# Gated delta-rule attention on one core: the correction of a triangular inverse summed in one bank, the unit matrix taken off by VectorE, and the inverse's steps moved

## Chip, core and metric

One core of a Trainium2 chip runs the whole program. The metric is device microseconds from start to end. One profiled execution gives the rows below; its own time stands beside its span in the table of the section on the profile.

## What is computed

The input has 2 sequences of 512 tokens, 256 wide. The first layer is linear attention with a gated delta rule: 16 key heads, 2 value heads to each, 128 wide. Cut to its core, the reference does for each value head and token

```python
def step(Sst, inp):
    q_t, k_t, v_t, g_t, beta_t = inp
    Sst = Sst * jnp.exp(g_t)[..., None, None]
    kv = jnp.einsum('bhk,bhkv->bhv', k_t, Sst)
    delta = (v_t - kv) * beta_t[..., None]
    Sst = Sst + k_t[..., None] * delta[:, :, None, :]
    o = jnp.einsum('bhk,bhkv->bhv', q_t, Sst)
    return (Sst, o)
```

Before it come a projection, a causal convolution of 4 taps and SiLU; behind it a normalisation, a gate SiLU(z) and an output projection. The second layer is a mixture of 12 experts, which the change doesn't touch.

## The kernel before

**Tiling.** Tokens are cut into chunks of 128, 4 to a sequence. For a key head there are 16 units (2 sequences, 4 chunks, 2 value heads), each with a 128 x 128 unit-triangular matrix A. The delta rule inside a chunk is a solve with A; the kernel makes an inverse Z of A and multiplies with it. A head is one pass of the whole program, and the units are worked in 4 groups of 4 (`g` 0 to 3, one PSUM bank of 512 columns each) or in 2 halves of 8.

**The inverse.** `aT` is A transposed; `aH` (fp16) and `aL` (the rest) are its parts. `st` starts an approximate inverse X0, `y`, `p` and `turn` widen it in 5 levels, with Z0 its transpose. Then comes one correction of higher order, which the change is about. With R the residual (unit matrix less A X0), Z = Z0 + R Z0 + R (R Z0):

- `res` (`residual`, L631 on TensorE): for each of the 4 units of a group, aH X0 + aL X0 (L640, L641) and a third product (L642) that takes the unit matrix off: `minus16` times `ident16`. ScalarE (L873) copies the bank with scale −1 to fp16, `res0`. VectorE (L1083) makes `res1`, the part that fp16 leaves out, in bf16.
- `once` (`apply_once`, L645): res0 Z0 into a bank of its own (L651); ScalarE (L877) copies it to fp16.
- `Z` (`finish_z`, L654): into a further bank, four products for each unit: res0 `once`, res1 Z0, res0 Z0 again, and the unit matrix times Z0 (L660 to L663). ScalarE (L881) copies it to `Z` in fp32.

**The recurrence.** For chunks c = 0 to 3 in turn: `ks c` (products with the state St, TensorE L687; VectorE L1094 makes `rh` of it), `solve c` (Z times rh, L704; ScalarE L904 copies to `dl`), `su c` (L713; VectorE updates St, L1102 for c = 0 and L1108), `pdl` and `qs` for the output.

**Order.** Every engine runs its steps in one written order: `FIRST`, then `ORDER` once for each of the heads 1 to 12, then `LAST` (L39 to L276). An entry (a, step, x) of `ORDER` is done for head w + a, so that three heads overlap. `run` gives each engine those entries that it has a part in, in the order of the list. `BANK` gives the PSUM bank of each step (banks 2 to 7). `full` and `free` of a bank count its uses; `is_full` waits until TensorE has filled it, `is_free` until its reader is done. Semaphores beside them count the tiles in SBUF (`res_high`: res0 is made).

**VectorE's order around the change.** In a head of `ORDER`, with the heads' number left out: `p (2,1)`, `y (4,0)`, `tap 1`, `y (3,1)`, `pdl 3`, `p (4,0)`, `sum 2`, `sum 3`, `norm`, `p (3,1)`, `tap 2`, `weigh 0`, `tok 0`, `tok 1`, `y (4,1)`, `weigh 1`, `p (4,1)`, `tap 3`, `weigh 2`, `weigh 3`, `res 0`, `op 0`, `tap 0`, `res 1`, `op 1`, `res 2`, `op 2`, `op 3`, `kk 0`, `aT 0`, `kk 1`, `aT 1`, `split z`, `split out`, `res 3`, `kk 2`, `st 0`, `su 0`, `st 1`, `aT 2`, `ks 1`. The lines: `tap` is L1023, `weigh` L1143, `op` L1150, `kk` L1054 (mask of a bank), `aT` L1060 (the factor: kkm times decay, both in SBUF), `split z` L1007, `split out` L1013 (fp32 weights less their fp16 part, both in SBUF), `st` L1066, `y` L1072, `p` L1081. TensorE's order from `ks 1` on: `ks 1`, `y (0,0)`, `x0 0`, `kk 3`, `solve 1`, `once 3`, `p (0,0)`, `qs 1`, `st 2`, `su 1`, and so on to `y (2,1)`, `turn (1,1)`, `p (3,0)`, `proj 1`, `p (2,1)`. GpSimd's: `gl 3`, `pT 0` (L1187, from kkm and decay), `unit 0`, `unit 1` (L1193, writes ones on the diagonal of aT), `aL 0` (L1199, the low part), `pT 1`, `aL 1`, `unit 2`, ...; `unit g` waits for the factor `aT g`, `aL g` for ScalarE's aH, and `aT 2` comes in VectorE's order behind `st 1`.

## Time and profile before

| | us |
|---|---|
| Runs: median of 3 (lowest, highest) | 1452.8 (1451.58, 1452.94) |
| The profiled execution's own time | 1452.13 |
| Its span, first to last instruction | 1450.4 |
| TensorE busy | 1386.4 (96%) |
| VectorE busy | 1085.8 (75%) |
| ScalarE busy | 1049.7 (72%) |
| GpSimd busy | 697.1 (48%) |
| Attention, about | 0 to 1104 |

PE is TensorE, PEld its weight load, DVE VectorE, ACT ScalarE, POOL GpSimd. A row of a group gives the line, engine, operation, output and inputs with shapes, how often, busy time and the mean of one in ns, and behind the second bar the idle time before. Matmul rows overlap their neighbours, since a matmul's row runs to the end of its pipeline; the distance of two starts is what it takes of the engine. A VectorE row of 0.68 us also overlaps the next by some 0.09.

### The profile page before, as it was taken

The numbers are of one execution on the slowest core, as the hardware profiler recorded it, in microseconds if no ns is written. First come the engines' busy times: TensorE is split into PE (matmuls) and PEld (weight loads), VectorE is DVE, ScalarE is ACT, GpSimd is POOL, SyncE is SP. The second block draws the span as 40 slices with busy tenths as digits, with TensorE's granted clock in tenths as the row PEclk, the third lists the DMA queues.
The fourth block names the chain that finished last, engine by engine and source line by source line (L and its number), as shares of the span: only waits on it lengthen the run. The fifth ranks groups of instructions, "written<-read, shape, count | busy, mean of one in ns | idle before, by whom it ended". The sixth has DMA issues, their size and how long they took to land.

```text
span 1450.4 us, 36480 instructions
## 1 busy us (share of the span) xinstructions
PE 1386.4 (96%) x14236; PEld 1114.9 (77%) x14236; DVE 1085.8 (75%) x1926; ACT 1049.7 (72%) x2114; POOL 697.1 (48%) x619
## 2 busy tenths in 40 slices
PE   5689999999999999999999999999978999999996
PEld 3568888898888889798888979888865567667676
DVE  5678999999999999999999999998865512213225
ACT  5777887878788787878888887887755465564651
POOL 0545555446564545556454555545315454353440
PEclk8899999999999999999999999999998999999998
DMA  3000202011020211102030110201131112112100
GB/s 118 16 1 2 67 3 58 24 38 38 24 60 2 60 24 38 38 25 59 2 60 18 44 38 24 60 2 39 32 101 39 56 37 73 38 37 73 37 1 29
DMA packets 100992, 55.76 MB, mean 38 GB/s; under 512 B 74572, under 2 KB 93016, under 8 KB 100824
## 3 DMA queue, kind: packets, MB, share of 16 engines
q1 hardware_dynamic: 100824, 53.43, 14.2%
q8 instruction: 116, 1.90, 0.5%
q14 instruction: 52, 0.43, 0.1%
HBM read 35.59 MB, written 1.05 MB: 25 GB/s over the span
## 4 chain that ended last, share of the span: by engine, by line
PE 89%; DVE 5%; ACT 2%; issue 2%; DMA 1%; POOL 0%; SPq 0%; POOLq 0%; DVEq 0%; ACTq 0%
PE bank L532 11%; PE bank L1486 11%; PE bank L1469 11%; PE bank L687 6%; PE bank L733 5%; PE bank L674 5%; PE bank L704 4%; PE bank L722 4%; PE bank L713 3%; PE bank L622 2%; PE bank L614 2%; PE bank L630 2%; PE bank L582 2%; PE bank L558 2%; PE bank L583 2%; DVE con L1023 2%
## 5 line engine op out<-in xcount | busy, mean ns | idle before, releaser
L1023 DVE SCALAR_TENSOR_TENSOR con<-bank,taps,con 128x1022 f32<-128x1022 f32 (+2 forms) x192 | 245.4, 1278 | 19.9 <-ACT con L802 15.3
L1808 POOL TENSOR_TENSOR h<-h 128x512 f16<-128x512 f32 x120 | 142.5, 1192 | 159.7 <-ACT h L1586 147.7
L532 PE MATMUL bank<-x,qkv 128*128 128x512 f16 x768 | 183.5, 390 | 6.5 <-DVE con L1023 6.5
L1179 POOL TENSOR_TENSOR gl<-const_sb,gc 128x512 f16<-128x512 f32 x128 | 129.9, 1040 | 120.3 <-DVE gc L1033 75.2
L1585 ACT ACTIVATE h<-bank,b 128x512 f32<-128x512 f32 x120 | 82.5, 687 | 119.0 <-PE bank L1469 115.8
L1469 PE MATMUL bank<-y,w 128*128 128x512 f16 x720 | 163.2, 386 | 1.7 <-ACT h L1586 1.4
L1486 PE MATMUL bank<-w,h 128*128 128x256 f16 x1440 | 159.9, 273 | 0.0
L1486 PEld LDWEIGHTS bank<-w,h 128*128 128x128 f16 x1440 | 140.9, 98 | 18.4
L532 PEld LDWEIGHTS bank<-x,qkv 128*128 128x128 f16 x768 | 73.4, 100 | 88.5 <-issue 8.7
L1469 PEld LDWEIGHTS bank<-y,w 128*128 128x128 f16 x720 | 70.2, 99 | 90.6 <-ACT h L1586 8.1
L1214 POOL TENSOR_TENSOR oo<-oo 128x512 f16<-128x512 f32 x64 | 74.2, 1170 | 122.0 <-ACT oo L930 122.0
L1081 DVE TENSOR_TENSOR X<-X,bank 128x512 f16<-128x512 f16 x160 | 109.0, 682 | 16.1 <-PE bank L622 14.7
L1399 DVE SCALAR_TENSOR_TENSOR w<-w,w 128x1280 f16<-128x1280 f32 x12 | 17.8, 1490 | 134.1 <-ACT w L1387 134.1
L871 ACT ACTIVATE Z<-bank 128x512 f16<-128x512 f32 x160 | 96.4, 604 | 23.7 <-PE bank L630 23.7
L1072 DVE TENSOR_TENSOR Y<-bank,ymask 128x512 f16<-128x512 f32 x160 | 109.4, 685 | 2.9 <-PE bank L614 2.3
L802 ACT ACTIVATE con<-bank,taps 128x512 f32<-128x512 f32 x128 | 85.4, 687 | 30.8 <-PE bank L532 30.6
L1206 POOL TENSOR_TENSOR kd<-k_tok,gc 128x512 f32<-128x512 f32 x48 | 50.0, 1043 | 112.0 <-PE bank L713 112.0
L733 PE MATMUL bank<-out,sqo 128*128 128x256 f16 x768 | 96.7, 277 | 7.2 <-ACT zs L889 5.5
L1187 POOL TENSOR_TENSOR pT<-kkm,decay 128x512 f32<-128x512 f32 x64 | 88.0, 1376 | 17.4 <-issue 12.8
L1709 DVE SCALAR_TENSOR_TENSOR facc<-bank,gcol,facc 128x256 f32<-128x256 f32 x88 | 38.5, 479 | 76.6 <-PE bank L1486 76.6
L674 PE MATMUL bank<-z,x 128*128 128x256 f16 x768 | 89.6, 273 | 1.4 <-ACT zs L889 0.8
L733 PEld LDWEIGHTS bank<-out,sqo 128*128 128x128 f16 x768 | 73.3, 99 | 22.1 <-issue 8.7
(222 smaller groups left out, 3858.2 us busy)
## 6 DMA issues: line engine op xcount, KB each, us to landing
w<-in_w SPq DMA_DIRECT2D x24, 640.0 KB, 4.4
w_qkv<-in_W_qkvz SPq DMA_DIRECT2D x16, 512.0 KB, 4.3
w_out<-in_W_out SPq DMA_DIRECT2D x16, 256.0 KB, 3.0
w_z<-in_W_qkvz SPq DMA_DIRECT2D x16, 256.0 KB, 2.9
Z<-in_xT SPq DMA_DIRECT2D x2, 512.0 KB, 5.5
y<-in_x SPq DMA_DIRECT2D x1, 1024.0 KB, 7.8
sqo<-oo SPq DMA_TRANSPOSE x64, 2.7
out_dram<-y SPq DMA_DIRECT2D x8, 128.0 KB, 1.8
```

The source lines that it names most:

```text
L532: last = mm(bank[:, b], qkv16[:, w, a, t * P:(t + 1) * P], x16[:, x, a, b * S:(b + 1) * S], start=(a == k == 0), stop=(a == HT - 1 and k = ...
L674: last = mm(out[:, j * 256:(j + 1) * 256], x16[:, x, a, m * P:(m + 1) * P], z16[:, w, a, :], start=(a == k == 0), stop=(a == HT - 1 and k ...
L733: last = mm(out[:, j * H:(j + 1) * H], oT[:, g % 2, o, 2 * j + r], out16[:, w, r, :], start=(r == i == 0), stop=(r == R - 1 and i == len(P ...
L871: freed(do(dst, src, ACT.Copy), "turn", lh)
L1023: stt(out=out, in0=bank[:, 0:B, 0:S - k], scalar=taps[:, par, t, TAPS - 1 - k:TAPS - k], in1=out, op0=ALU.mult, op1=ALU.add).then_inc(tap_ ...
L1072: freed(tt(Y[:, h], at_bank("y", lh).rearrange("p (u k) -> p u k", u=8), ymask[:, l].unsqueeze(1).broadcast_to([P, 8, P // 2]), ALU.mult), ...
L1081: freed(tt(x, x, at_bank("p", lh).rearrange("p (q b) -> p q b", b=b), ALU.subtract), "p", lh)
L1179: last = tt(gl[:, g % 2, k].rearrange("p (m r) d -> p m r d", m=2), upper.unsqueeze(1).unsqueeze(1).broadcast_to([P, 2, R, P]), gc[:, par, ...
L1187: tt(pT[:, par, 4 * g:4 * g + 4].rearrange("p (m r) d -> p m r d", m=2), kkm[:, g % 2, :, 1].unsqueeze(2).broadcast_to([P, 2, R, P]), deca ...
L1469: last = mm(h_bank(n, k), w1_16[:, n % 2, w, a, t * P:(t + 1) * P], y16[:, x, a, h * S:(h + 1) * S], start=(a == i == 0), stop=(a == HT - ...
L1486: last = mm(o_bank(k)[:, j * H:(j + 1) * H], h16[:, n % 2, h, t, m * P:(m + 1) * P], w2_16[:, n % 2, w, t, :], start=(t == i == 0), stop=( ...
L1808: tt(h16[:, n % 2, 1, t, at], h32[:, k % H32], h16[:, n % 2, 0, t, at], ALU.subtract).then_inc(h_low, 1)
```

## The change

Six things change.

1. TensorE's `residual` leaves out the product with `minus16`: 2 products for a unit instead of 3.
2. VectorE makes `res0` itself, with one instruction that scales the bank by −1 and adds the unit matrix (fp16, broadcast over the 4 units), and waits for it (`res_high`) before `res1` from the same bank. `res1` is −(A X0) less res0 as before, so it now differs from R's rest by the unit matrix. ScalarE's `residual` is gone.
3. The correction is summed in the bank of `once`. `apply_once` starts it (only its first product has the start flag), ScalarE copies R Z0 out, and `finish_z` adds to the same bank: res0 `once`, res1 Z0, and `twice16` (twice the unit matrix) times Z0; the second unit matrix answers to what `res1` now has too little of. The second res0 Z0 is left out: 3 products for a unit instead of 4.
4. `Z` needs no bank of its own, so four entries of `BANK` go, and `p (4,1)` and `once 2` get other banks.
5. Semaphores `once_ready` and `z_full`, four of each, take the place of bank waits between these steps.
6. The orders are rewritten. In `ORDER`, VectorE's steps differ in two places: `res 1` comes before `tap 0`, and `res 3` between `aT 0` and `kk 1` instead of behind `split out`. On TensorE, `res 1` comes before `proj 0`, `once 2` behind `op 3`, `res 3` right behind `kk 0`, `Z 2` and `once 1` behind `kk 1`, `Z 3` before `st 3`, `y (4,1)` before `z 1`, `y (3,1)` before `decay 0`, `turn (1,0)` behind `y (2,0)`. On ScalarE, `once 2` is last, and `v (1,1)` comes before `turn (1,0)`. GpSimd's and the DMA queue's orders stay, but for the list's cut (`aL 3` is first of a head instead of last of the one before). `FIRST` and `LAST` are rewritten more widely, in the same manner.

```diff
@@ ORDER: the entries around the moved steps
-    (1, "aT", 1), (0, "split", "z"), (0, "split", "out"), (0, "Z", 2),
-    (0, "once", 1), (0, "res", 3), (1, "aH", 0), (1, "kk", 2),
...
+    (0, "res", 3), (1, "kk", 1), (1, "aT", 1), (0, "split", "z"),
+    (0, "split", "out"), (0, "Z", 2), (0, "once", 1), (1, "aH", 0),
...
@@ tensor: residual, apply_once, finish_z, solve
                 mm(out[:, at], aH[:, u], X0[:, u], start=True, stop=False)
-                mm(out[:, at], aL[:, u], X0[:, u], start=False, stop=False)
-                last = mm(out[:, at], minus16[:], ident16[:], start=False, stop=True)
+                last = mm(out[:, at], aL[:, u], X0[:, u], start=False, stop=True)
             filled(last, "res", g)
...
             for j in range(4):
-                last = mm(out[:, j * P:(j + 1) * P], res0[:, g, j], Z0[:, 4 * g + j], start=True, stop=True)
+                last = mm(out[:, j * P:(j + 1) * P], res0[:, g, j], Z0[:, 4 * g + j], start=(j == 0), stop=True,
+                          skip_group_check=True)
             filled(last, "once", g)
...
-            is_free(pe, n, ("res", g), ("once", g), taking=("Z", g))
-            out = take(n, "Z", g)
+            pe.wait_ge(once_ready[g], n + 1)
+            is_free(pe, n, ("res", g))
+            out = at_bank("once", g)
             for j in range(4):
                 u, at = 4 * g + j, slice(j * P, (j + 1) * P)
-                mm(out[:, at], res0[:, g, j], once[:, g % 2, j], start=True, stop=False)
-                mm(out[:, at], res1[:, g, j], Z0[:, u], start=False, stop=False)
-                mm(out[:, at], res0[:, g, j], Z0[:, u], start=False, stop=False)
-                last = mm(out[:, at], ident16[:], Z0[:, u], start=False, stop=True)
-            filled(last, "Z", g)
+                mm(out[:, at], res0[:, g, j], once[:, g % 2, j], start=False, stop=False, skip_group_check=True)
+                mm(out[:, at], res1[:, g, j], Z0[:, u], start=False, stop=False, skip_group_check=True)
+                last = mm(out[:, at], twice16[:], Z0[:, u], start=False, stop=True, skip_group_check=True)
+            last.then_inc(z_full[g], 1)
...
-                needs += [("Z", c // 2), ("Z", 2 + c // 2)]
+                needs += [("once", c // 2), ("once", 2 + c // 2)]
@@ scalar
         def turn_start(n, par, h):
-            is_full(act, n, ("x0", h), ("Z", 2 * h, 1), ("Z", 2 * h + 1, 1))
+            is_full(act, n, ("x0", h))
+            if after(n, 1):
+                act.wait_ge(z_full[2 * h], n)
+                act.wait_ge(z_full[2 * h + 1], n)
...
-        def residual(n, par, g):
-            is_full(act, n, ("res", g), ("Z", g, 1))
-            do(res0[:, g], quads(at_bank("res", g)), ACT.Copy, scale=-1.0).then_inc(res_high, 1)
-
         def apply_once(n, par, g):
-            is_full(act, n, ("once", g), ("Z", g - 2) if g >= 2 else ("Z", g + 2, 1))
-            freed(do(once[:, g % 2], quads(at_bank("once", g)), ACT.Copy), "once", g)
+            is_full(act, n, ("once", g))
+            if g >= 2:
+                act.wait_ge(z_full[g - 2], n + 1)
+            elif after(n, 1):
+                act.wait_ge(z_full[g + 2], n)
+            do(once[:, g % 2], quads(at_bank("once", g)), ACT.Copy).then_inc(once_ready[g], 1)
 
         def finish_z(n, par, g):
-            is_full(act, n, ("Z", g), ("solve", 2 * (g % 2) + 1, 1))
-            freed(do(Z[:, 4 * g:4 * g + 4], quads(at_bank("Z", g)), ACT.Copy), "Z", g)
+            act.wait_ge(z_full[g], n + 1)
+            is_full(act, n, ("solve", 2 * (g % 2) + 1, 1))
+            freed(do(Z[:, 4 * g:4 * g + 4], quads(at_bank("once", g)), ACT.Copy), "once", g)
@@ vector
-            ts(minus16[:], ident, -1.0, None, ALU.mult)
+            ts(twice16[:], ident, 2.0, None, ALU.mult)
...
         def residual(n, par, g):
+            is_full(dve, n, ("res", g))
+            if after(n, 1):
+                dve.wait_ge(z_full[g], n)
+            stt(out=res0[:, g], in0=quads(at_bank("res", g)), scalar=-1.0,
+                in1=ident16[:].unsqueeze(1).broadcast_to([P, 4, P]), op0=ALU.mult, op1=ALU.add).then_inc(res_high, 1)
             dve.wait_ge(res_high, 4 * n + g + 1)
             freed(stt(out=res1[:, g], in0=quads(at_bank("res", g)), scalar=-1.0, in1=res0[:, g],
                       op0=ALU.mult, op1=ALU.subtract), "res", g)
```

## Rows read from the trace of the kernel before

**Rows 1.** The page, part 1: busy time, share and count.
```profile
PE 1386.4 (96%) x14236; PEld 1114.9 (77%) x14236; DVE 1085.8 (75%) x1926; ACT 1049.7 (72%) x2114; POOL 697.1 (48%) x619
```

**Rows 2.** Busy time by stretches: length, engines, granted clock, DMA share, GB/s.
```profile
400.60:464.50 63.90, 63.78 (x747) 54.72 (x745) 59.74 (x105) 52.50 (x114) 34.12 (x31) 1.00 0.14 35
...
976.00:1040.00 64.00, 62.71 (x760) 54.99 (x759) 56.44 (x107) 49.36 (x109) 28.26 (x25) 1.00 0.11 27
```

**Rows 3.** Groups by line, whole span: products that go, ScalarE's step, its neighbour.
```profile
L662 PE MATMUL bank<-Z,res 128*128 128x128 f16 x256 | 56.1, 219 | 0.0
...
L642 PE MATMUL bank<-ident,minus 128*128 128x128 f16 x256 | 46.0, 219 | 0.0
...
L1085 DVE SCALAR_TENSOR_TENSOR res<-bank,res 128x512 bf16<-128x512 f32 x64 | 43.4, 683 | 10.1 <-ACT res L875 10.1
...
L875 ACT ACTIVATE res<-bank 128x512 f16<-128x512 f32 x64 | 38.6, 603 | 13.1 <-PE bank L642 12.6
```

**Rows 4.** TensorE in order of time: start us, duration us, what.
```profile
416.70 0.22 PE L640 MATMUL bank<-X,aH 128*128 128x128 f16 x1
...
417.31 0.22 PE L642 MATMUL bank<-ident,minus 128*128 128x128 f16 x1
...
433.34 1.03 PE L687 MATMUL bank<-St,kT 128*128 128x256 f32 x4
...
455.66 0.40 PE L622 MATMUL bank<-Y,Z 128*128 128x64 f16 x8
```

**Rows 5.** VectorE in order of time, with the waits.
```profile
415.91 0.69 DVE L1085 SCALAR_TENSOR_TENSOR res<-bank,res 128x512 bf16<-128x512 f32 x1 [0.51 <-ACT res L875]
...
417.58 3.91 DVE L1023 SCALAR_TENSOR_TENSOR con<-bank,taps,con 128x1022 f32<-128x1022 f32 x3 [0.38 <-ACT con L802]
...
424.64 0.69 DVE L1054 TENSOR_TENSOR kkm<-bank,const_sb 128x512 f32<-128x512 f32 x1 [0.16 <-PE bank L583]
425.37 0.69 DVE L1060 TENSOR_TENSOR aT<-kkm,decay 128x512 f32<-128x512 f32 x1
425.98 0.68 DVE L1054 TENSOR_TENSOR kkm<-bank,const_sb 128x512 f32<-128x512 f32 x1
426.69 1.05 DVE L1060 TENSOR_TENSOR aT<-kkm,decay 128x512 f32<-128x512 f32 x1
427.67 1.12 DVE L1007 SCALAR_TENSOR_TENSOR z<-w_z,z 128x512 f16<-128x512 f32 x1
428.71 1.12 DVE L1013 SCALAR_TENSOR_TENSOR out<-w_out,normw,out 128x512 f16<-128x512 f32 x1
429.75 0.68 DVE L1085 SCALAR_TENSOR_TENSOR res<-bank,res 128x512 bf16<-128x512 f32 x1
430.35 0.67 DVE L1054 TENSOR_TENSOR kkm<-bank,const_sb 128x512 f32<-128x512 f32 x1
...
431.94 0.69 DVE L1102 COPY St<-bank 128x512 f32<-128x512 f32 x1 [0.25 <-PE bank L713]
...
433.14 0.68 DVE L1060 TENSOR_TENSOR aT<-kkm,decay 128x512 f32<-128x512 f32 x1
434.40 1.13 DVE L1094 SCALAR_TENSOR_TENSOR rh<-bank,gc,v_tok 128x128 f32<-128x128 f32 x4 [0.58 <-PE bank L687]
...
456.09 0.69 DVE L1081 TENSOR_TENSOR X<-X,bank 128x512 f16<-128x512 f16 x1 [0.47 <-PE bank L622]
```

**Rows 6.** GpSimd in order of time over the same steps.
```profile
425.47 1.73 POOL L1187 TENSOR_TENSOR pT<-kkm,decay 128x512 f32<-128x512 f32 x1 [0.91 <-issue]
427.14 2.13 POOL L1193 TENSOR_SCALAR_AFFINE_SELECT aT<-aT 128x512 f32<-128x512 f32 x2
429.25 1.59 POOL L1199 TENSOR_TENSOR aL<-aT,aH 128x512 f16<-128x512 f32 x1
...
432.03 1.16 POOL L1199 TENSOR_TENSOR aL<-aT,aH 128x512 f16<-128x512 f32 x1
```

**Rows 7.** The z split's line alone: durations ns min/median/max over 16 heads.
```profile
L1007 DVE SCALAR_TENSOR_TENSOR z<-w_z,z x16: 681/1118/1445, 98.2 to 1073.2; 128x512 f16<-128x512 f32 x16
```

More of the change, by code:

```diff
@@ new lines @@
+    (15, "load", "out"), (14, "sum", 1), (14, "sqo", 2), (14, "solve", 3),
+    (14, "sum", 2), (15, "turn", (3, 0)), (15, "turn", (2, 1)), (15, "y", (3, 1)),
[3 rows of a table added]
+    (14, "weigh", 0), (15, "turn", (3, 1)), (14, "z", 2), (14, "weigh", 1),
+    (14, "high", 0), (14, "weigh", 2), (14, "z", 3), (15, "norm", 0),
+    (14, "high", 1), (15, "p", (4, 1)), (14, "high", 2), (15, "turn", (4, 0)),
+    (15, "res", 0), (15, "res", 1), (15, "pT", 3), (15, "turn", (4, 1)),
[4 rows of a table added]
+    (14, "low", 0), (15, "once", 1), (14, "op", 2), (14, "high", 3),
@@ L323, in attention @@
     pT = sb("pT", [P, 2, U, P])
-    minus16 = sb("minus16", [P, P], F16)
+    twice16 = sb("twice16", [P, P], F16)
     unit_cols = sb("unit_cols", [P, LEVELS, P // 2], F16)
@@ L370, in attention @@
         "proj_full", "tap0_done", "tap_done", "silu_done", "sq_done", "rs_ready"))
+    once_ready, z_full = ([sem(f"{name}{g}") for g in range(4)] for name in ("once_ready", "z_full"))
     scaled = sem("scaled")
```

201 lines of the change are left out of this document (107 added, 94 removed), and 236 rows, old and new, of tables (BANK, FIRST, LAST, ORDER).

## Prediction

> **What bounds the kernel now.** I read the views from wide to narrow: the page, then busy time by stretches, then the groups by line, then the order in time of TensorE, VectorE and GpSimd over one head. The page puts TensorE at 96% of the span [rows 1]. By stretches [rows 2], the middle of the kernel repeats every 63.9 us: the stretch shown is one of 13 alike between 145 and 976 us. TensorE is busy 63.78 of 63.90 us there at a granted clock of 1.00 (its 2.4 GHz level), and VectorE 59.74 us. So TensorE is the bound of a head and VectorE is only 4 us behind. In the last full stretch but one of attention, 976 to 1040 us, both have a little room. The experts (from 1104 us on) are not touched.
>
> **What goes from TensorE.** In `residual` the product with `minus16`, in `finish_z` the second product of res0 with Z0: 4 each per step, 4 steps a head, 16 heads, 512 products of 128 columns [rows 3]. Their price is not the 219 ns of a row, which overlap, but the distance of starts: from the first product of a `res` step to its twelfth there are 11 steps in 0.61 us [rows 4], 55.6 ns each. A head saves 32 x 0.0556 = 1.78 us, the kernel 28.5 us, if TensorE stays the bound. By the Trainium skill (TensorE: Matmul & The Clock Gate, Back-to-back issue gap) pairs of load and matmul of 128 columns are sustained at about 81 ns, which would make it 41.5 us; the rows are shorter, and they decide.
>
> **What moves.** ScalarE loses `residual`, 64 x 0.60 us [rows 3]; it is busy 52.5 us a head [rows 2] and only waits less. VectorE gets that step as a `scalar_tensor_tensor` of one bank. Nothing in the trace is this very instruction; the nearest row is L1085, same engine and opcode, same bank and 512 elements, 0.68 us [rows 3]. In its queue such an instruction takes less, since the next starts before it ends (429.75 to 430.35, 0.60), but its partner res1 needs its result at once. That is the spacing of the mask product and the factor behind it, 425.98 to 426.69, 0.71 us [rows 5]. I take 0.71; 0.60 is the low end and 1.1 (a blocked instruction, 428.71 below) the high end. Four a head: **+2.84 us**, 2.4 to 4.4. `twice16` for `minus16` and the flags of the products cost nothing: same instructions, same count. The extra pair of waits on z_full is met long before: a Z step stands most of a head ahead of the next `res` of its group. Evacuations of `once` and `Z` are the same instructions from one bank instead of two.
>
> **Where that lies.** VectorE needs 59.7 + 2.8 = 62.5 us a head and TensorE 62.1: they are now equals, and what counts is how they hand over. The loop of a head that sets the end has three pieces, in the clock of [rows 4] and [rows 5].
> (a) VectorE's own queue, from the instruction `p (2,1)` that waits for TensorE at 456.09 to the state copy at 431.94 of the next head (495.84): 39.75 us. VectorE waits four times in it: 0.51, 0.38, 0.16 and, at the copy itself, 0.25.
> (b) From the copy to the `ks 1` products that read the state, 433.34: 1.40 us, of which the copy is 0.69. The rest is TensorE's queue.
> (c) TensorE's queue from `ks 1` to `p (2,1)` at 455.66, and 0.43 to VectorE's start: 22.75 us.
> Together 63.90.
> In (a) all four `res` pairs lie, +2.84. With VectorE late, its four waits go: 1.30, and 0.09 more for each (0.69 of duration against 0.60 of spacing), 1.66. Moving `res 3` ahead of `kk 1` and taking ScalarE's part out remove the wait for ScalarE. Net +1.18, so the copy is no longer waiting for the products of `su 0`, and TensorE, now about 1.5 us ahead, waits for the copy: (b) falls to 0.69 + 0.06 = 0.75, −0.65. (c) loses the four products of `Z 3`: −0.22. `once 2`, moved behind `op 3`, will wait about a microsecond for res0, which falls in TensorE's spare time. Sum so far +0.31, a head of 64.2.
>
> **The port.** There is one more term in (a). The second factor `aT` takes 1.05 us at 426.69, and the two weight splits 1.12 each at 427.67 and 428.71 [rows 5]; the same z split takes 0.68 when nothing runs beside it [rows 7]. All three read two operands from SBUF. Each begins while a GpSimd instruction is under way, the pT product (425.47) and the two unit selects (427.14) [rows 6], and ends some 0.55 us after that one: whoever starts first holds the other up. Factors that start ahead of GpSimd (425.37) take 0.69. L1085 and the mask products read one bank and at most one SBUF operand, and never stretch, so the new instruction doesn't either. The Trainium skill says the same (SBUF — State Buffer, Who interferes with whom): a VectorE instruction with two SBUF inputs and a GpSimd one that reads SBUF block each other for a whole instruction, by order of issue. The trace agrees, with 1.12 against 0.68.
> In the new order `res 3` (1.31 us) stands between the first factor and `kk 1`. GpSimd finishes pT and the first select before the second factor starts (pT 426.3 to 428.0, select to 428.6, factor 428.8), so that takes 0.69; the z split starts right behind it, before the second select that waits for the factor, and takes 0.68; the out split is still blocked. **−0.36 −0.44 = −0.80**. The loop: 63.90 + 0.31 − 0.80 = **63.4 us a head**; over 13 heads −6.4 us.
>
> **The ends.** Attention's first 145 us and last 128 us hold three heads' work outside this loop, with a rewritten order. Saved products are worth at most 3 x 1.78 = 5.3 us there; added VectorE work costs at most 3 x 2.84 = 8.5. From 976 to 1040 us VectorE is busy 56.4 us of 64 [rows 2], so products saved in head 14 and in head 15 up to its first solve should show by about half of 3.6: I take −2, ends −5.3 and +4. The three solves behind them alternate between engines and don't change. Sum: −6.4 − 2 = −8.4 us on the profiled execution's 1452.1 us, 1443.7; the median of runs stands 0.7 us above that execution, so **1444 us**.
>
> **Rivals.**
> 1. *TensorE stays the bound.* All 28.5 us come off: 1424. For it: TensorE is full now. Against: VectorE's 62.5 us leave no room for heads of 62.1 us. 0.06, with 0.05 for cases in between.
> 2. *The relief at the port is given back one instruction later.* With pT, the selects and the low parts about 1.3 us later on GpSimd than now ([rows 6]: low parts at 429.25 and 432.03), its second low part starts at about 433.3, and the factor `aT 2`, which now starts at 433.14 clear of it, would start at 433.5 and wait a whole low part: 1.5 us instead of 0.69. That puts `ks 1`'s evacuation and `solve 1` some 0.6 us later: 64.0 us a head, +1.3 over 13, with the ends and the median's 0.7 1452. It hangs on 0.2 us. 0.19.
> 3. *Slower: VectorE's queue is the bound and the port gives nothing.* From the place between `res 0` and `ks 1`, +0.31 a head as summed above, or +0.9 with rival 2 on top: 1452.8 + 4 = 1457 up to 1465. It decides as soon as the port gives back less than 0.31 us a head. For it: 2.84 us go to the engine with 4 us left, and those four microseconds are mostly waits that the recurrence forces (0.58 before `ks 1` [rows 5]). The Trainium skill warns of this side (Perfetto Trace Analysis, Optimizing Scalar/DVE Operations): with VectorE saturated, work should go to ScalarE, and the change goes the other way. 0.25.
> That the change doesn't do what it says can be told by counts alone, and I see no way for it.
>
> **How the numbers follow.** Forecast 0.46; partial cases between it and rival 1 0.05; rival 1 0.06; rival 2 0.19; rival 3 0.24. Faster by over 0.2% (2.9 us, about what a measurement can tell): the forecast, the partial cases and rival 1, 0.57. Within 0.2%: rival 2, 0.19. Slower: rival 3, 0.24. The forecast's own range is 1438 to 1449 (ends ±4, port ±0.1 a head). To leave out 2 in 10 the range takes in rivals 2 and the nearer part of 3 and leaves out rival 1: 1434 to 1459.
>
> **What would show it.** Right: heads of 63.4 us; TensorE busy near 62 us a head with gaps in front of `once 2` and `ks 1`; VectorE without waits from `p (2,1)` to the state copy; the new instruction at 0.68 and 0.71 ahead of res1; the second factor and the z split at 0.69; `aT 2` at 0.68. Wrong in size: any of the three SBUF products at 1.05 or more. Wrong in kind: heads of 62.1 us with VectorE still waiting, or TensorE's gaps at another step than those two.

## Result, and the profile after

The kernel became slower: median 1471.2 us (1469.34 to 1471.79, 4 runs) against 1452.6 us of the kernel before in the same comparison, a ratio of 1.0128 [1.0112, 1.0144]. The forecast of 1444 and its range, 1434 to 1459, both missed. The profiled execution took 1471.79 us, its span 1470.0 us, 19.6 us more than before.

The page's line of busy times, which answers to [rows 1], and the shares of the chain that ended last, by engine:

```profile
PE 1369.1 (93%) x13724; PEld 1087.7 (74%) x13724; DVE 1132.2 (77%) x1990; ACT 1020.9 (69%) x2050; POOL 691.6 (47%) x619
...
PE 62%; DVE 22%; issue 8%; ACT 6%; POOL 1%; DMA 1%; SPq 0%; DVEq 0%; POOLq 0%; ACTq 0%
```

The same line of the chain in the kernel before:

```profile
PE 89%; DVE 5%; ACT 2%; issue 2%; DMA 1%; POOL 0%; SPq 0%; POOLq 0%; DVEq 0%; ACTq 0%
```

The counts are those of the diff: 512 products fewer on TensorE, 64 instructions more on VectorE and 64 fewer on ScalarE. What changed in kind is the chain: it ran through TensorE for 89% of the span and now passes from engine to engine.

**Where the 19.6 us are.** One row per head tells it, VectorE's first copy of the state, whose instruction waits for the recurrence. It first runs at 111.66 us before and 118.55 after: +6.9 in the opening. From this copy to the last one (15 distances, opening and closing heads among them) it is 945.0 us before and 959.1 after: +14.1. Behind the last copy it is −1.30. A middle head, 63.90 before, is 65.12, where 63.4 was forecast. (For every kernel below I give these two figures, first copy and middle head.)

The stretches of [rows 2] again, start and end, then length, then busy time of PE, PEld, DVE, ACT, POOL, then the granted clock, DMA share and GB/s:

```profile
0.00:80.00 80.00, 51.48 (x379) 34.96 (x379) 46.92 (x71) 50.57 (x90) 24.90 (x30) 0.83 0.19 61
80.00:145.00 65.00, 56.86 (x607) 44.72 (x607) 52.15 (x84) 43.90 (x97) 25.24 (x26) 0.92 0.02 6
400.60:464.50 63.90, 61.45 (x700) 51.91 (x697) 61.68 (x106) 50.42 (x109) 33.60 (x30) 1.00 0.16 35
```

TensorE is now idle 2.45 us in these 63.9, and VectorE is as busy as TensorE. TensorE in order of time, those rows of one middle head that have a wait in front of them (in brackets, us and what ended it), and two that mark the loop's pieces:

```profile
415.45 0.39 PE L615 MATMUL bank<-X,aH 128*128 128x64 f16 x8 [0.96 <-ACT Z L875]
...
422.30 1.48 PE L675 MATMUL bank<-z,x 128*128 128x256 f16 x12 [0.31 <-DVE X L1086]
...
433.59 1.47 PE L734 MATMUL bank<-out,sqo 128*128 128x256 f16 x12 [0.78 <-ACT Z L888]
...
441.74 1.13 PE L705 MATMUL bank<-v_tok,Z 128*128 128x128 f32 x8 [0.40 <-DVE kkm L1059]
...
446.58 1.03 PE L688 MATMUL bank<-St,kT 128*128 128x256 f32 x4
```

Four waits stand where the kernel before had hardly any, and none of them is where the prediction put one (`once 2` and `ks 1`). They are `y (4,1)`, `z 3`, `op 2` and `solve 0`. Each waits for a bank whose reader has not yet come to it: `y (4,1)` needs bank 2, which held `turn (4,0)` (ScalarE's L875 reads it); `z 3` needs bank 4 of `p (4,1)`; `op 2` needs bank 2, which `once 0` now keeps until `Z 0` is out; `solve 0` needs bank 4 of `kk 1`, whose mask VectorE now makes behind `res 3`.

VectorE in order of time over the same head; it answers to [rows 5]:

```profile
403.88 0.69 DVE L1086 TENSOR_TENSOR X<-X,bank 128x512 f16<-128x512 f16 x1 [0.47 <-PE bank L623]
...
419.43 2.00 DVE L1153 SCALAR_TENSOR_TENSOR oo<-oo,rso,zs 128x128 f32<-128x128 f32 x4
421.56 0.69 DVE L1086 TENSOR_TENSOR X<-X,bank 128x512 f16<-128x512 f16 x1
...
428.08 0.69 DVE L1092 SCALAR_TENSOR_TENSOR res<-bank,ident 128x512 f16<-128x512 f32 x1
428.80 0.69 DVE L1095 SCALAR_TENSOR_TENSOR res<-bank,res 128x512 bf16<-128x512 f32 x1
...
441.63 0.69 DVE L1065 TENSOR_TENSOR aT<-kkm,decay 128x512 f32<-128x512 f32 x1
442.24 0.69 DVE L1012 SCALAR_TENSOR_TENSOR z<-w_z,z 128x512 f16<-128x512 f32 x1
442.84 1.12 DVE L1018 SCALAR_TENSOR_TENSOR out<-w_out,normw,out 128x512 f16<-128x512 f32 x1
...
445.18 0.69 DVE L1112 COPY St<-bank 128x512 f32<-128x512 f32 x1
...
446.39 1.50 DVE L1065 TENSOR_TENSOR aT<-kkm,decay 128x512 f32<-128x512 f32 x1
```

The loop's pieces in these rows, beside the forecast: (a) from `p (2,1)` at 403.88 to the state copy at 445.18 it is 41.30 us (40.13 forecast); (b) from there to `ks 1` at 446.58 it is 1.40 (0.75 forecast); (c) from `ks 1` to the next `p (2,1)`, 469.01, it is 22.43 (22.53 forecast). Their sum is 65.13.

The row that stands out is 2.00 us for `weigh 1`. The row of GpSimd beside it, and the row of ScalarE on which `y (4,1)` waited:

```profile
414.65 0.65 ACT L875 ACTIVATE Z<-bank 128x512 f16<-128x512 f32 x1
...
419.33 1.16 POOL L1224 TENSOR_TENSOR oo<-oo 128x512 f16<-128x512 f32 x1 [2.28 <-ACT oo L935]
```

GpSimd's low part of `oo` starts 0.10 us ahead of `weigh 1`, and `weigh 1` takes 2.00 in place of 1.13. The ScalarE copy at 414.65 stands right behind the eight squares of `sq1`. So the suspicion was a chain: `y (4,1)`, moved ahead of `z 1`, waits 0.96 us for bank 2; `z 1` and all behind it (`high 0`, then GpSimd's `low 0`) come late; `low 0` meets `weigh 1`.

The first half of this holds, and the second half costs nothing. The chain that ended last, in order of time (start, us, what; the same head), leads from ScalarE's copy through TensorE's own queue to VectorE's `p (4,1)`, the row at 421.56, and leaves `weigh 1` out:

```profile
414.82 0.50 ACT Z L875
...
415.45 0.39 PE bank L615 x8
415.84 2.62 PE bank L675 x24
...
421.29 0.25 PE bank L623 x8
421.56 0.69 DVE X L1086
```

`weigh 1` ends at 421.43, and VectorE then still waits 0.13 us for TensorE's `p (4,1)`. Without the collision it would have waited 1.00 us there. So what makes the head longer is TensorE's wait, which reaches `p (4,1)` undiminished; the 2.00 us are hidden behind it.

### The profile page after: what moved, and what is told of

Read it like the earlier page. It is cut to its first block, busy times and chain, and to the rows that moved or that the text cites. A ratio compares the mean times of both kernels' runs of the same rounds, so it can differ in the third digit from the quotient of the medians.

```text
span 1470.0 us, 35518 instructions
## 1 busy us (share of the span) xinstructions
PE 1369.1 (93%) x13724; PEld 1087.7 (74%) x13724; DVE 1132.2 (77%) x1990; ACT 1020.9 (69%) x2050; POOL 691.6 (47%) x619
## 4 chain that ended last, share of the span: by engine, by line
PE 62%; DVE 22%; issue 8%; ACT 6%; POOL 1%; DMA 1%; SPq 0%; DVEq 0%; POOLq 0%; ACTq 0%
PE bank L1496 11%; PE bank L1479 10%; DVE con L1028 8%; PE bank L533 7%; PE bank L688 6%; PE bank L705 3%; PE bank L723 3%; PE bank L714 3%; PE bank L675 3%; PE bank L615 2%; DVE res L1092 2%; DVE y L1160 2%; PE bank L623 2%; DVE oo L1153 2%; ACT sq L825 2%
## 5 line engine op out<-in xcount | busy, mean ns | idle before, releaser
L1028 DVE SCALAR_TENSOR_TENSOR con<-bank,taps,con 128x1022 f32<-128x1022 f32 (+2 forms) x192 | 245.3, 1278 | 18.8 <-ACT con L803 14.1
L875 ACT ACTIVATE Z<-bank 128x512 f16<-128x512 f32 x160 | 96.5, 604 | 27.9 <-PE bank L631 27.9
```

The source lines that it names most:

```text
L875: freed(do(dst, src, ACT.Copy), "turn", lh)
L1028: stt(out=out, in0=bank[:, 0:B, 0:S - k], scalar=taps[:, par, t, TAPS - 1 - k:TAPS - k], in1=out, op0=ALU.mult, op1=ALU.add).then_inc(tap_ ...
```

## Experiments

Seventeen kernels ran beside the kernel before and the changed one. "Order" in the edits is the list `ORDER`, in which one entry stands for one step on all engines.

### The parts alone

**vector_only**: the kernel before, its orders and banks, with the VectorE part alone (`Z` keeps its own bank and the second product res0 Z0).

```diff
-                mm(out[:, at], aL[:, u], X0[:, u], start=False, stop=False)
-                last = mm(out[:, at], minus16[:], ident16[:], start=False, stop=True)
+                last = mm(out[:, at], aL[:, u], X0[:, u], start=False, stop=True)
@@ vector: residual, ahead of res1
+            stt(out=res0[:, g], in0=quads(at_bank("res", g)), scalar=-1.0,
+                in1=ident16[:].unsqueeze(1).broadcast_to([P, 4, P]), op0=ALU.mult, op1=ALU.add).then_inc(res_high, 1)
@@ scalar: residual is out; twos for ones in finish_z
```

> The kernel before with one part of the change: the product with the negative unit matrix goes, VectorE makes res0, ScalarE's step goes; order, banks and the four products of the Z step (the last with twice the unit matrix) as before. Theory 1 (load): VectorE's queue from p (2,1) to the state copy is on the loop that sets the end, and the 2.84 us a head put there come out less the waits they fill (1.66): heads of 64.3 to 65.2 us, 1457 to 1470 us in all. Theory 2 (order and bank): the loss comes from the rewritten order and from the bank that is held from the once step to the end of the Z step; neither is in this kernel, so that it stands at 1440 to 1453 us.

Measured: 1544.9 us, 1.0635 [1.0599, 1.0671]; first copy 113.51, heads of 69.4 and 70.5 us in turn. Neither theory came near it. TensorE in one of them:

```profile
455.52 0.60 PE L650 MATMUL bank<-Z,res 128*128 128x128 f16 x4 [4.00 <-DVE res L1080]
```

In the old order `once 2` comes soon after `res 2` on TensorE, while VectorE's `res 2` stands behind a tap step of 3.9 us. ScalarE had no such step in front of it. So the moves are no ornament: with the old order the VectorE part costs 92 us. But the run doesn't give this part's own price, since the wait drowns it.

**sum_only**: the changed kernel, its orders, banks and one-bank sum, with the residual as it was (product with `minus16`, ScalarE's copy).

```diff
-                last = mm(out[:, at], aL[:, u], X0[:, u], start=False, stop=True)
+                mm(out[:, at], aL[:, u], X0[:, u], start=False, stop=False)
+                last = mm(out[:, at], minus16[:], ident16[:], start=False, stop=True)
@@ scalar: residual is back; vector: the new instruction is out; ones for twos in finish_z
```

> The changed kernel (its order, its banks, the correction summed in one bank, three products in the Z step) with the old residual: product with the negative unit matrix, ScalarE makes res0. TensorE 0.89 us a head lighter than before, VectorE as before. Theory 1 (load): TensorE is the bound again, heads of 63.0 to 63.3 us, 1438 to 1446 us. Theory 2 (order and bank): the new waits stay, heads of 64 us and more, 1455 to 1470 us.

Measured: 1475.2 us, 1.0155 [1.0125, 1.0184]; first copy 118.81, heads 65.22. TensorE and VectorE of it:

```profile
414.97 0.39 PE L615 MATMUL bank<-X,aH 128*128 128x64 f16 x8 [0.94 <-ACT Z L876]
...
421.82 1.48 PE L676 MATMUL bank<-z,x 128*128 128x256 f16 x12 [0.31 <-DVE X L1093]
...
433.77 1.47 PE L735 MATMUL bank<-out,sqo 128*128 128x256 f16 x12 [0.78 <-ACT Z L895]
```

```profile
418.96 1.97 DVE L1155 SCALAR_TENSOR_TENSOR oo<-oo,rso,zs 128x128 f32<-128x128 f32 x4
```

This is the run that turned the inquiry. VectorE carries nothing new here, and the head and the opening are as long as in the changed kernel, with three of its four waits and the blocked `weigh 1`. The changed kernel's loss is in the orders and banks, and not in VectorE's load: putting that load back (changed kernel against sum_only) makes a head 0.10 us shorter. The chain that ended last leaves `weigh 1` out here too, and VectorE waits 0.14 us for `p (4,1)` behind it.

### Which move

**y41_back**: the changed kernel with `y (4,1)` back behind `z 2` in `ORDER`.

```diff
-    (0, "z", 0), (1, "y", (4, 1)), (0, "z", 1), (2, "silu", 2),
-    (0, "high", 0), (0, "z", 2), (0, "low", 0), (0, "low", 1),
-    (0, "oT", 3), (0, "weigh", 1), (1, "turn", (3, 1)), (2, "proj", 3),
+    (0, "z", 0), (0, "z", 1), (2, "silu", 2), (0, "high", 0),
+    (0, "z", 2), (0, "low", 0), (0, "low", 1), (0, "oT", 3),
+    (1, "y", (4, 1)), (0, "weigh", 1), (1, "turn", (3, 1)), (2, "proj", 3),
```

> The changed kernel with y (4,1) moved back behind z 2 in the twelve middle heads. In the changed kernel TensorE waits 0.96 us for ScalarE ahead of y (4,1), z 1 and the ScalarE and GpSimd steps behind it come late, and weigh 1 on VectorE starts 0.1 us behind a GpSimd instruction: 2.00 us instead of 1.13. If VectorE's queue is on the loop (theory 1): the collision goes, heads of 64.2 to 64.4 us instead of 65.1, 1458 to 1462 us. Rival: another engine is on the loop there, and the 0.87 us are hidden: 1470 us within 2.

Measured: 1457.2 us, 1.0036 [1.0018, 1.0054]; first copy 117.59, heads 64.03. One entry moved back returns 14 of the 18.6 us, 1.09 a head. (In the two traces 12.3 us of it lie between the first and the last copy. Another 1.0 lies ahead of the first copy, where the two kernels' lists are the same, so that part is not the move's.) VectorE of it, then TensorE:

```profile
399.38 0.69 DVE L1086 TENSOR_TENSOR X<-X,bank 128x512 f16<-128x512 f16 x1 [0.47 <-PE bank L623]
...
414.92 1.13 DVE L1153 SCALAR_TENSOR_TENSOR oo<-oo,rso,zs 128x128 f32<-128x128 f32 x4
...
439.59 0.69 DVE L1112 COPY St<-bank 128x512 f32<-128x512 f32 x1
```

```profile
436.15 1.13 PE L705 MATMUL bank<-v_tok,Z 128*128 128x128 f32 x8 [0.41 <-DVE kkm L1059]
...
440.99 1.03 PE L688 MATMUL bank<-St,kT 128*128 128x256 f32 x4
```

`weigh 1` is back at 1.13, and (a) is 40.21 us, where 40.13 was forecast. (b) is still 1.40. The gain is the distance from `p (2,1)` to `p (4,1)` on VectorE: 16.60 us, as in the kernel before, for 17.67 in the changed one. The expectation put it down to the collision; but the edit takes TensorE's wait away together with the collision, and by the chain above the wait is what counted.

**y41_forward**: the reverse test, the kernel before with that one entry moved forward and nothing else changed.

```diff
-    (0, "z", 1), (2, "silu", 2), (0, "high", 0), (0, "z", 2),
-    (0, "low", 0), (0, "low", 1), (0, "oT", 3), (1, "y", (4, 1)),
+    (1, "y", (4, 1)), (0, "z", 1), (2, "silu", 2), (0, "high", 0),
+    (0, "z", 2), (0, "low", 0), (0, "low", 1), (0, "oT", 3),
```

> The kernel before with y (4,1) ahead of z 1 in the middle heads and nothing else. Both y (4,1) and turn (4,0) use bank 2, and ScalarE copies turn (4,0) only behind the eight squares of sq1. If this wait is the cost in itself: TensorE loses 0.9 to 1.1 us a head, 1463 to 1467 us. If it costs only together with VectorE's added work: 1453 to 1456 us.

Measured: 1464.5 us, 1.0083 [1.0068, 1.0098]; heads 64.98, +1.08. TensorE, then VectorE and GpSimd:

```profile
408.99 0.39 PE L614 MATMUL bank<-X,aH 128*128 128x64 f16 x8 [0.95 <-ACT Z L871]
```

```profile
412.98 1.98 DVE L1143 SCALAR_TENSOR_TENSOR oo<-oo,rso,zs 128x128 f32<-128x128 f32 x4
```

```profile
412.87 1.16 POOL L1214 TENSOR_TENSOR oo<-oo 128x512 f16<-128x512 f32 x1 [2.27 <-ACT oo L930]
```

The same wait, the same collision with the same lead (0.11 us), the same price. With and without the rest of the change this move costs 1.1 us a head, as the first theory had it. Here too the chain that ended last goes through the ScalarE copy and TensorE and leaves `weigh 1` out, and VectorE waits 0.14 us for `p (4,1)` behind it. No kernel was run that has the wait and not the collision.

**res1_back**: the changed kernel with `res 1` back behind `tap 0`.

```diff
-    (1, "res", 1), (2, "proj", 0), (1, "once", 0), (2, "tap", 0),
+    (2, "proj", 0), (1, "once", 0), (2, "tap", 0), (1, "res", 1),
```

> The changed kernel with res 1 moved back behind tap 0 on both engines in the twelve middle heads. VectorE's work is the same, but tap 0, and with it silu 0, decay 1 and ScalarE's steps up to the state copy, come 1.3 us sooner. Theory 1a (VectorE's queue alone sets the loop): 1470 us within 2. Theory 1b (VectorE up to tap 0, then ScalarE's chain of silu 0, table load, decay 1 and the splits, sets it): heads about 0.6 us shorter, 1461 to 1465 us. If the move was right: slower, 1472 or more.

Measured: 1478.3 us, 1.0176 [1.0147, 1.0206]; heads 65.58, +0.46, with a new wait of 0.36 us for VectorE's `res` ahead of `op 3`. It comes out behind the changed kernel, so this move was right for that kernel.

### The waits that were left

**banks_free**, **banks_port** and **port_free** start from y41_back. The first gives `op 2`, `op 3`, `res 3` and `p (4,1)` other banks; port_free puts `aL 1` behind `unit 2` in `ORDER`, so that GpSimd's low part no longer holds up VectorE's `aT 2`; banks_port does both.

```diff
@@ banks_free
-    ("res", 3): 2 ... ("p", (4, 1)): 4 ... ("op", 2): 2 ... ("op", 3): 7
+    ("res", 3): 7 ... ("p", (4, 1)): 6 ... ("op", 2): 7 ... ("op", 3): 2
@@ port_free
-    (1, "pT", 1), (1, "aL", 1), (1, "y", (1, 0)), (0, "pdl", 1),
-    (1, "unit", 2), (1, "aH", 3), (2, "load", "qkv"), (1, "turn", (0, 0)),
+    (1, "pT", 1), (1, "y", (1, 0)), (0, "pdl", 1), (1, "unit", 2),
+    (1, "aL", 1), (1, "aH", 3), (2, "load", "qkv"), (1, "turn", (0, 0)),
```

> The changed kernel with y (4,1) behind z 2 (as in y41_back) and four banks exchanged: op 2 in bank 7 instead of 2 (which the once step of group 0 now holds until the Z step's copy), op 3 and res 3 in 2 and 7, p (4,1) in 6. TensorE's waits of 0.78 us ahead of op 2 and 0.35 ahead of z 3 go. If VectorE's queue from p (2,1) to the state copy is the bound of y41_back's heads (it shows no wait there in 40.2 us), they are hidden: heads of 63.8 to 64.05 us, 1454 to 1458 us. If TensorE's waits are what is lost: heads 0.8 to 1.1 us shorter, 1442 to 1448 us.

> banks_free with GpSimd's low part aL 1 moved behind unit 2, so that VectorE's aT 2 finds the port free (0.69 us instead of 1.50). If piece (b) of the loop can shrink only when both TensorE and VectorE come early (ks 1 right behind the state copy, its evacuation not behind a blocked aT 2): heads 0.3 to 0.7 us shorter than banks_free, 1446 to 1452 us. Rival: TensorE reaches ks 1 no sooner, and only 0.2 us a head are gained, 1453 to 1456 us.

> y41_back with aL 1 behind unit 2 alone, banks as changed. The price of aT 2 behind a GpSimd instruction by itself: its evacuation rh of ks 1 starts 2.62 us behind the state copy and could start at 2.46, when ks 1's products end. 0.2 us a head: 1454 to 1456 us against y41_back's 1457. If the blocked instruction cost its full 0.81 us: 1446.

Measured: 1469.0 us, 1.0106 [1.0087, 1.0125]; 1468.0 us, 1.0099 [1.0083, 1.0115]; 1458.5 us, 1.0037 [1.0024, 1.0051]. In all three a middle head stays at 64.03. In banks_free and banks_port the wait of `z 3` is gone. That of `op 2` has only changed its cause and grown: the profile now puts it down to the DMA that transposes its input. TensorE of banks_free:

```profile
426.77 1.49 PE L734 MATMUL bank<-out,sqo 128*128 128x256 f16 x12 [1.44 <-DMA sqo<-oo]
```

The head is no shorter without the first and no longer with the second: TensorE had that time to spare. The kernel as a whole lost 12 us by these banks, most of it in closing heads of 65.5 and 72.3 where y41_back has 63.6 and 65.6, and 3 us behind the last copy. And with `aT 2` unblocked, which the next rows show, nothing is gained either:

```profile
440.04 0.69 DVE L1112 COPY St<-bank 128x512 f32<-128x512 f32 x1
...
441.25 0.68 DVE L1065 TENSOR_TENSOR aT<-kkm,decay 128x512 f32<-128x512 f32 x1
442.51 1.12 DVE L1104 SCALAR_TENSOR_TENSOR rh<-bank,gc,v_tok 128x128 f32<-128x128 f32 x4 [0.58 <-PE bank L688]
```

The factor takes 0.68 instead of 1.50, and VectorE then waits 0.58 us for `ks 1` instead. The blocked factor had stood in a gap. For banks_free the head was forecast (63.8 to 64.05) and the whole was not; for banks_port and port_free even the smallest gain named did not come.

**solve_bank** (y41_back with `solve 0` in bank 3) takes the wait for `kk 1` away, and **solve_port** adds port_free's move to it.

```diff
-    ("solve", 0): 4, ("decay", 2): 7, ("st", 0): 2, ("su", 0): 4, ("st", 1): 5,
+    ("solve", 0): 3, ("decay", 2): 7, ("st", 0): 2, ("su", 0): 4, ("st", 1): 5,
```

> y41_back with solve 0 in bank 3 (free there once the Z copies it needs are made) instead of bank 4, where it waits 0.41 us for VectorE's mask of kk 1, which the change put behind res 3. Theory: the loop of y41_back's heads closes over this wait: kk 1 on VectorE, then TensorE's solve 0, decay 2, Z 1, st 0, su 0, pdl 0, decay 3, ks 1. Then ks 1 comes up to 0.4 us sooner, but its evacuation stays behind the blocked aT 2: 0.0 to 0.1 us a head, 1456 to 1458 us. If the blocked aT 2 doesn't hold: 0.3 to 0.5 a head, 1451 to 1453.

> solve_bank with aL 1 behind unit 2 on GpSimd, so that aT 2 isn't blocked. If both hold piece (b) of the loop together, only this one is shorter: heads of 63.5 to 63.7 us instead of 64.03, 1450 to 1453 us. If VectorE's queue with the ends of PE's work is the whole bound: 64.03 again, 1457 us.

Measured: 1458.4 us, 1.0041 [1.0025, 1.0057], heads 64.03; and 1456.0 us, 1.0024 [1.0014, 1.0034], heads 63.78. TensorE and VectorE of solve_port:

```profile
438.57 1.02 PE L688 MATMUL bank<-St,kT 128*128 128x256 f32 x4
```

```profile
437.32 0.68 DVE L1112 COPY St<-bank 128x512 f32<-128x512 f32 x1
...
439.63 1.13 DVE L1104 SCALAR_TENSOR_TENSOR rh<-bank,gc,v_tok 128x128 f32<-128x128 f32 x4 [0.44 <-PE bank L688]
```

Neither edit alone gives anything. In solve_bank (b) is already 1.25 and (a) 0.10 shorter, but (c) grows from 22.41 to 22.66, and `aT 2` freed takes that back. TensorE must be early for `ks 1` and VectorE free for what follows; both together give 0.25 us a head. Of the wait of 0.41 us ahead of `solve 0` about half is left, at `st 1` (0.22 us), which waits for VectorE's mask of `kk 2`. This is the best form of the whole change that I ran, and it is not faster than the kernel before.

### The one-bank sum without the VectorE part

**sum_banks**: sum_only with `y (4,1)` back and the banks of banks_free. **sum_lean**: the kernel before with its own orders and only the one-bank sum (`once 2` in bank 3, `op 2` in 5, `decay 1` in 2, and five steps moved in the opening and the closing where a bank forced it). **sum_lean2**: the same with two steps moved, for the waits that sum_lean showed: `split out` behind `res 3`, and `turn (4,1)` in bank 6 and, in opening and closing, later.

```diff
@@ sum_lean2 against sum_lean
-    (1, "aT", 1), (0, "split", "z"), (0, "split", "out"), (0, "Z", 2),
-    (0, "once", 1), (0, "res", 3), (1, "aH", 0), (1, "kk", 2),
+    (1, "aT", 1), (0, "split", "z"), (0, "Z", 2), (0, "once", 1),
+    (0, "res", 3), (0, "split", "out"), (1, "aH", 0), (1, "kk", 2),
```

> sum_only (old residual with ScalarE's res0, three products in the Z step) with y (4,1) behind z 2 and the same exchange of banks as banks_free. If the new waits of TensorE ahead of y (4,1), op 2 and z 3 were what made sum_only slow: TensorE is the bound with 63.0 us of work a head, heads of 63.1 to 63.6 us, 1444 to 1451 us with the seven us lost before the middle heads. If holding the bank costs elsewhere too: heads of 64 us, 1457 us or more.

> The kernel before (its orders and banks) with the sum in one bank alone: three products in the Z step instead of four, residual as before. Five steps moved in the opening and the end and none in the middle heads; once 2 in bank 3, op 2 in 5, decay 1 in 2, so that nobody waits for a bank that once holds. If the loss of sum_only came from the changed order and from op 2's bank: TensorE stays the bound with 0.89 us less a head: heads of 63.0 us, 1437 to 1442 us, faster than both. If holding the once bank or reading it twice costs in itself: heads of 63.5 or more, 1446 or more.

> sum_lean with turn (4,1) in bank 6 and ahead of op 1 in the opening and the end (instead of ahead of once 0), and with split out behind res 3 in the middle heads, so that VectorE reads res 3's bank a microsecond sooner and st 0 doesn't wait. If saved products are worth their spacing once no wait takes their place: heads of 63.0 to 63.2 us, 1440 to 1446 us, faster than both kernels. If something else holds the head: 63.6 again, 1449 us or more.

Measured: 1460.0 us, 1.0048 [1.0033, 1.0063], heads 63.43; 1457.8 us, 1.0037 [1.0023, 1.0051], heads 63.67; 1454.0 us, 1.0017 [1.0008, 1.0026], heads 63.66.

**What VectorE's part is worth.** sum_banks and banks_free have the same orders and banks and differ in the residual alone. The heads are 63.43 and 64.03, the whole 1460.0 and 1469.0 us: with these banks VectorE's part costs 0.60 us a head, all of it in (a), 39.61 against 40.22. With the banks of the change it costs nothing: sum_first (below) has heads of 64.14 where first_back and y41_back, with VectorE's part, have 64.03. The waits for banks had hidden it.

sum_banks has the shortest heads of all runs, as forecast, and not the time forecast with them: its first copy is at 118.58 us and its closing heads take up to 68.0.

**What the saved products are worth.** TensorE has 16 products, 0.89 us, less to do in a head, and the heads of the two lean kernels are 0.24 us shorter. In sum_lean (a) is 39.73 us, unchanged, and (c) is 22.53 for 22.75. That is the forecast's −0.22 for the four products of `Z 3`. The other twelve lie in (a) and give nothing, as TensorE and VectorE of sum_lean show:

```profile
437.27 0.38 PE L594 MATMUL bank<-ident,aH 128*128 128x128 f16 x4 [0.57 <-DVE res L1097]
```

```profile
438.64 0.69 DVE L1114 COPY St<-bank 128x512 f32<-128x512 f32 x1 [0.25 <-PE bank L715]
```

TensorE reaches `st 0` early and waits there for VectorE to empty the bank of `res 3`, so that the state copy behind it comes no sooner. All four waits of [rows 5] in (a) are still there. In sum_lean2, VectorE and then TensorE, the one at the copy is gone and the other three stay; the last row of VectorE is the first of them a head later:

```profile
418.31 0.69 DVE L1097 SCALAR_TENSOR_TENSOR res<-bank,res 128x512 bf16<-128x512 f32 x1 [0.52 <-ACT res L882]
...
419.99 3.91 DVE L1035 SCALAR_TENSOR_TENSOR con<-bank,taps,con 128x1022 f32<-128x1022 f32 x3 [0.39 <-ACT con L804]
...
427.04 0.69 DVE L1066 TENSOR_TENSOR kkm<-bank,const_sb 128x512 f32<-128x512 f32 x1 [0.16 <-PE bank L584]
...
481.97 0.69 DVE L1097 SCALAR_TENSOR_TENSOR res<-bank,res 128x512 bf16<-128x512 f32 x1 [0.52 <-ACT res L882]
```

```profile
434.10 0.38 PE L594 MATMUL bank<-ident,aH 128*128 128x128 f16 x4 [0.53 <-DVE kkm L1066]
```

VectorE's waits for ScalarE, 0.51 and 0.38 before, are 0.52 and 0.39: they don't shrink when TensorE gets lighter. The wait of 0.25 at the state copy went, but it bought nothing: (b) is 1.25, (a) is 39.87, and the head is that of sum_lean, where the wait is still there. TensorE waits 0.53 us for VectorE's mask instead. So with this order a loop of about 63.66 us, through VectorE and ScalarE in (a), stood right behind TensorE's 63.9; with that of sum_banks it is 63.43. Both lean kernels fall where their expectations put the other case, and as a whole they also lose outside the middle heads. In sum_lean the first distance between copies is 71.5 us for 64.6; in sum_lean2 the first copy is at 114.19, and a closing head takes 67.6 for 64.05.

### The opening

**first_back**: y41_back with the opening order of the kernel before, three of its steps moved for the banks. **first_bank**: that with `p (4,1)` in bank 6. **sum_first**: sum_only with `y (4,1)` back and that opening. **vector_moved**, for the other question left, is vector_only with the change's moves of `once 2`, `res 1` and `res 3`.

```diff
@@ first_back, sum_first: the list FIRST of the kernel before, and
-GATE_BANKS = (3, 2)
+GATE_BANKS = (4, 2)
@@ first_bank
-    ("p", (4, 1)): 4
+    ("p", (4, 1)): 6
@@ vector_moved
-    (1, "kk", 0), (1, "load", "z"), (1, "aT", 0), (1, "kk", 1),
+    (1, "kk", 0), (1, "load", "z"), (1, "aT", 0), (0, "res", 3), (1, "kk", 1),
...
-    (1, "once", 0), (2, "tap", 0), (1, "res", 1), (0, "op", 1),
+    (1, "res", 1), (2, "proj", 0), (1, "once", 0), (2, "tap", 0), (0, "op", 1),
...
-    (1, "once", 2), (1, "kd", 1), (2, "silu", 0), (1, "aL", 3),
+    (1, "kd", 1), (2, "silu", 0), (1, "aL", 3), (0, "op", 2), (2, "decay", 1), (0, "op", 3), (1, "once", 2),
```

> y41_back with the opening order (heads 0 and 1, up to the middle heads) of the kernel before, but for three steps moved so that a bank held from once to Z is not needed in between. The changed kernel reaches head 0's first state copy 6.9 us later than the kernel before. If the rewritten opening is what costs them: 6 to 8 us less than y41_back, 1449 to 1452 us. If VectorE's added work and the held bank cost them: within 2 us of y41_back, 1455 to 1459.

> first_back with p (4,1) in bank 6 as in the kernel before. Read by the first state copy and the first two heads, not by the whole time, since the closing order conflicts with that bank (banks_free lost 8 us there). If the new opening order is what costs: first copy at 112 to 113 us. If VectorE's added work costs: 115 to 118 us.

> sum_only (the part of the change that takes a product out of the Z step and leaves the residual as it was) with y (4,1) behind z 2 and the opening of first_back, banks as changed. Middle heads of 63.4 to 63.7 us (TensorE 63.0 us of work, and its wait ahead of op 2), the opening as before: 1442 to 1448 us, faster than both kernels. Rival: the held bank costs in the opening and heads stay at 64: 1452 or more.

> vector_only (VectorE makes res0 and takes the unit matrix off; four products in the Z step) with three of the change's moves in the middle heads: once 2 last, res 1 ahead of proj 0, res 3 ahead of kk 1; y (4,1) stays where it was. The wait of 4 us ahead of once 2 goes. By the loop worked out for the prediction VectorE's queue from p (2,1) to the state copy is 40.1 to 40.2 us and the head 63.9 to 64.2: 1455 to 1466 us with the opening and the end, whose order isn't adapted. If VectorE had room: 63.0 a head, 1445 or less.

Measured:

| Kernel | median us, ratio | first copy | next distance |
|---|---|---|---|
| first_back | 1471.5, 1.0134 [1.0119, 1.0149] | 116.75 | 79.00 |
| first_bank | 1466.0, 1.0093 | 114.64 | 75.65 |
| sum_first | 1462.2, 1.0070 [1.0055, 1.0085] | 114.55 | 71.4 |
| before | | 111.66 | 64.60 |
| changed | | 118.55 | 65.88 |

These three are slow by my own doing: where the old opening meets the new head, a bank is taken twice. TensorE in first_back:

```profile
165.91 2.72 PE L734 MATMUL bank<-out,sqo 128*128 128x256 f16 x12 [5.09 <-DVE X L1086]
...
181.55 0.61 PE L651 MATMUL bank<-Z,res 128*128 128x128 f16 x4 [3.50 <-DVE res L1092]
```

So none of them is a better kernel, but the first copy lies ahead of these conflicts and can be read. sum_only and sum_lean do the same work, the one in the new opening order and banks and the other in the old ones (but for the few steps named): 118.81 and 112.36 us. The changed kernel, with the new work on VectorE, is no later than sum_only, at 118.55. One trace places the first copy only to about a microsecond: y41_forward has the opening of the kernel before unchanged and comes at 112.93 for 111.66. In four pairs of kernels that differ by VectorE's part alone, that part moves the first copy by +1.9 (vector_only against the kernel before), +2.2 (first_back against sum_first), −0.3 (changed against sum_only) and −2.4 (banks_free against sum_banks), so it has no reading of its own. The 6.9 us are the new opening's order and banks for the most part. They can't be split further: with my own banks in it the old opening gives 114.55 to 116.75, and kernels with the new one, which differ only behind it in their lists, come at 116.2 to 118.8. first_bank's 114.64 lies between the two figures that its expectation named, and decides nothing. Which step of the list it is was not tried.

vector_moved: 1517.0 us, 1.0447 [1.0431, 1.0462], heads of 67.9 us, two of them 66.6. A wait of 2.93 us for ScalarE's `decay 1`, which shares bank 5 with `once 2`, is ahead of `once 2`; its move needs its new bank too. So the VectorE part has no clean run in the old order.

## Why the prediction was wrong, point by point

**What the step is.** "In (a) all four `res` pairs lie" and the sums around it priced what VectorE executes. Of the steps moved on TensorE only `once 2` got a sentence, and `y (4,1)` ahead of `z 1` got none. The bank table was there to read: `turn (4,0)` and `y (4,1)` share bank 2 before and after, and the copy that frees it stands behind the squares of `sq1` in ScalarE's order. y41_back and y41_forward show that this costs 1.09 and 1.08 us a head. It lies in (a), between VectorE's `p (2,1)` and `p (4,1)`: 17.67 us with the move, in the changed kernel, and 16.60 without it. TensorE's wait of 0.96 is what delays `p (4,1)`; VectorE's blocked `weigh 1` looked like the price and was hidden. Over the whole kernel the move is 12 to 14 of the 18.6 us.

**The ends.** "I take −2" was sized from products saved, at most 5.3, and VectorE's added work, at most 8.5. The opening alone gave +6.9. Its rewritten order was taken as neutral; sum_only shows it is not. In the closing the last distance between copies is 46.4 us for 49.5, the two before it are together 2.6 us longer, and behind the last copy it is −1.30: a gain of 1.8 us in all, close to the 2 taken. What was mis-sized is the opening.

**Piece (a), VectorE's queue.** This was right once the move is out of the way: 40.21 us in y41_back against 40.13. The new instruction takes 0.68 (median of 64) and is followed after 0.72 by res1, for 0.71 forecast. The waits for ScalarE and TensorE are gone from `p (2,1)` to the copy. The second factor is 0.69 and the z split 0.69, so the port did give back what was forecast; the out split is still 1.12.

**Piece (b).** "TensorE, now about 1.5 us ahead, waits for the copy" was wrong: it stayed at 1.40 in the changed kernel and y41_back. VectorE's order puts `kk 1` behind `res 3`, and `solve 0` needs that bank, so TensorE waits 0.40 there and arrives no earlier. solve_bank and solve_port, with this mended, got to 1.25, not to 0.75. This term, 0.65, is about the whole difference between 63.4 and 64.03.

**Piece (c).** 22.43 against 22.53: right.

**Rival 2.** The mechanism came as told, with `aT 2` blocked at 1.50 us, and with no effect by itself: port_free has it at 0.68 and the same head. What it would have delayed was not ready before then. Once `ks 1` is early it costs 0.25 us a head (solve_bank against solve_port), where 0.6 was told.

**Rival 3.** The sign was its sign, and the reason was not. With y41_back, VectorE is the fuller engine and the heads are 64.03, about the +0.31 that it gave (64.2); but sum_only, with no VectorE work added, is as slow as the changed kernel. VectorE's part does cost, 0.60 us a head, where the banks are free (banks_free against sum_banks); in the changed kernel that was hidden. (The rival stands at 0.25 in its own item and at 0.24 in the sum of chances, which needs 0.24.)

**Rival 1, and what lay under all.** TensorE at 63.78 of 63.90 us looked like the bound, and its own saving looked like the ceiling. sum_lean took 0.89 us from TensorE and nothing else, and got 0.24 back, in (c). Of VectorE's four waits in (a), which I counted as slack of 1.30 us, 0.89 are for ScalarE and don't shrink when TensorE gets lighter. The two for TensorE, 0.16 and 0.25, stay as well, since TensorE itself then waits 0.57 us for VectorE.

**Left open.** The VectorE part's worth in the old order, since both kernels with it there carried another wait; which steps of the opening cost its 6.9 us; and whether an order exists with which the change wins. No kernel that I ran beats the kernel before: the nearest are sum_lean2, 1.0017 [1.0008, 1.0026], and solve_port, 1.0024.

## What to carry to other kernels

Price a moved step by its PSUM bank first: who read that bank last, what stands ahead of that reader in its own queue, and who is behind the moved step; one entry ahead of its time cost here more than all the added instructions. Before taking a 99% busy engine as the bound, look for the loop through the other engines, and ask in which piece of it the saved work lies: four products in TensorE's own stretch came back in full, twelve in VectorE's stretch not at all. A row that has become long is not yet a cost: look whether its engine still waits behind it, and whether the chain that ended last passes through it. A price found among other waits, or none, can change once they are gone: VectorE's added work cost nothing with one set of banks and 0.60 us a head with another. Test a change with rewritten orders with the new orders and the old work, as well as the old order and the new work: here the first told the cause, and in the second a new wait drowned it.
